# A graph layer and a 16-expert layer on one core: W centred in place of x, pads and b1 spread out, expert numbers loaded behind products

## What is computed

```python
deg = max((adj != 0).sum(-1), 1)                      # adj: 4096 x 4096, 0 or 1
xn = layernorm(x)                                     # x: 4096 x 256, over the 256, no gain or shift
x1 = x + relu((dinv * (adj + I) * dinv) @ xn @ W + xn @ W + b)   # dinv = rsqrt(deg), per row and its own degree
f = layernorm(x1)
w, idx = top_2(softmax(f @ Wr + br)); w = w / w.sum()
y = f + sum over the two chosen experts e of w_e * (gelu(f @ W1[e] + b1[e]) @ W2[e] + b2[e])
out = x1 + y
```

## Time and profile before

| | |
|---|---|
| median of 3 runs | 645.96 us |
| the profiled execution's own time | 647.67 us |
| its span, first to last instruction | 646.1 us |
| TensorE busy (products) | 585.0 us, 91% |
| VectorE busy | 456.3 us, 71% |
| ScalarE busy | 248.7 us, 38% |
| GpSimd busy | 307.2 us, 48% |
| DMA traffic | 94.60 MB, mean 146 GB/s |
| mean granted TensorE clock | 0.975 |

### The profile page before, as it was taken

The page is one execution under the profiler, slowest core; times in us unless marked ns, Lnnn a source line. Parts: engine busy times, 40 slices in busy tenths (PEclk is TensorE's granted clock), DMA queues, the critical chain, the costliest instruction groups (busy, mean ns, idle before and its releaser), DMA issues.

```text
span 646.1 us, 17010 instructions
## 1 busy us (share of the span) xinstructions
PE 585.0 (91%) x4732; PEld 459.4 (71%) x4733; DVE 456.3 (71%) x1433; ACT 248.7 (38%) x515; POOL 307.2 (48%) x348
## 2 busy tenths in 40 slices
PE   1998999999999999999717999899999999999993
PEld 1687888888888888888604666566666777777772
DVE  2664899999999999999733766667755565555662
ACT  2786343444344443444312344343332323233331
POOL 7213366666666666663320333544534443444443
PEclk9999999999999999999957999999999999999998
DMA  8916899999999999995593545666544443434320
GB/s 232 226 26 108 165 196 211 217 205 214 207 212 198 222 210 208 209 218 141 195 337 97 129 112 122 142 143 137 119 72 70 82 82 61 78 62 79 63 51 1
DMA packets 67450, 94.60 MB, mean 146 GB/s; under 512 B 9232, under 2 KB 42288, under 8 KB 66896
## 3 DMA queue, kind: packets, MB, share of 16 engines
q0 software_dynamic: 32928, 51.03, 45.6%
q1 hardware_dynamic: 32176, 40.32, 21.2%
q10 hardware_dynamic: 2304, 2.72, 1.3%
HBM read 103.71 MB, written 25.83 MB: 201 GB/s over the span
## 4 chain that ended last, share of the span: by engine, by line
PE 32%; DMA 5%; issue 5%; DVE 4%; ACT 2%; SPq 1%; POOLq 1%; DVEq 1%; POOL 0%
PE bank L584 13%; PE bank L607 11%; PE bank L592 4%; DMA out_dram<-orows,at_xg 4%; PE bank L562 2%; DVE hgs L1143 1%; ACT xseT L775 1%; PE bank L601 1%; DVE feat L1132 1%; DMA rows<-pad 1%; DMA at_xg<-rows 1%; DVE orows L1157 1%; DVE hl L1149 1%; SPq L336 0%; DVEq L1137 0%
## 5 line engine op out<-in xcount | busy, mean ns | idle before, releaser
L480 PE MATMUL bank<-wall,at_xg 128*128 128x257 f16 x1024 | 238.7, 273 | 1.9 <-DVE at_xg L842 1.6
L482 PE MATMUL bank<-wall,at_xg 128*128 128x256 f16 x1024 | 233.4, 273 | 0.0
L1322 POOL DMA_INDIRECT out_dram<-orows,at_xg x79 | 128.1, 1621 | 182.3 <-DMA out_dram<-orows,at_xg 101.2
L584 PE MATMUL bank<-wall,feat 128*128 (+1 forms) x474 | 118.0, 386 | 11.1 <-issue 8.3
L769 ACT ACTIVATE hgs<-hgs 128x512 f32<-128x512 f32 x79 | 49.8, 630 | 201.2 <-DVE hgs L1143 201.2
L1149 DVE SCALAR_TENSOR_TENSOR hl<-bank,xseT 128x512 f16<-128x512 f32 x79 | 54.6, 692 | 92.1 <-ACT xseT L775 92.1
L480 PEld LDWEIGHTS bank<-wall,at_xg 128*128 128x128 f16 x1024 | 102.9, 100 | 18.4 <-DVE at_xg L842 5.0
L1291 POOL DMA_INDIRECT rows<-feat,posi x64 | 72.7, 1136 | 85.4 <-issue 82.7
L482 PEld LDWEIGHTS bank<-wall,at_xg 128*128 128x128 f16 x1024 | 100.3, 98 | 15.3
L607 PE MATMUL bank<-wall,xseT 128*128 (+1 forms) x632 | 108.2, 273 | 0.0
L842 DVE STREAM_TRANSPOSE at_xg<-abuf 128x512 int32<-128x512 int32 x128 | 87.0, 698 | 3.9
(11 more groups left out here) (148 smaller groups left out, 768.1 us busy)
## 6 DMA issues: line engine op xcount, KB each, us to landing
abuf<-in_adj_dram POOLq DMA_DIRECT2D x128, 256.0 KB, 6.5
wst<-in_L_ffn_W_dram SPq DMA_DIRECT2D x32, 512.0 KB, 7.4
at_xg<-rows SPq DMA_DIRECT2D x79, 136.0 KB, 2.1
out_dram<-orows SPq DMA_DIRECT2D x32, 128.0 KB
abuf<-in_L_ffn_b_dram SPq DMA_DIRECT2D x4, 1024.0 KB, 9.8
wall<-in_x_dram SPq DMA_DIRECT2D x12, 256.0 KB, 13.4
rows<-pad ACTq DMA_DIRECT2D x12, 136.0 KB, 3.2
out_dram<-orows,at_xg POOLq DMA_INDIRECT x79, 3.9
```

What stands on the lines that cost most here:

```text
L480: both = [lambda: pe.matmul(ps_acc[odd][:, 0:D + 1], w, yh[:, j, 0:D + 1], start=j == 0, stop=j == T - 1), lambda: pe.matmul(ps_acc[odd][: ...
L482: lambda: pe.matmul(ps_acc[odd][:, 0:D], w, yl[:, j, :], start=False, stop=False)]
L584: mm = pe.matmul(q_h[r % 2][:, :], a, w, start=n == 0, stop=n == 3 * DC - 1)
L1322: L.indirect_dma_start(out, bass.IndirectOffsetOnAxis(ap=info[r][:, 0:1].bitcast(U32), axis=0), orow[r], None, bounds_check=N - 1, oob_is_ ...
```

## The change

First tile: x is no longer normalised before the product. TensorE makes the column means of W (`column_means`), VectorE subtracts them from W (`centre_W`), x is transposed as it arrives, and 1/sqrt of the variance multiplies y when it is copied out (`high_y`, `low_y`). Statistics run six tiles ahead (`LEAD`) in groups of 2, 3, 3 and then 4 tiles (`GROUPS`). W is the first load of SP; y has three banks in place of two; GpSimd makes the identity matrix before its first adjacency loads and issues those of tiles 1 to 3 from the first stage.

Turn: a block of pads is written early behind the start of each of the first eight experts' regions (`first_pads`), and those experts' own pads go behind their first block at the earliest (`pad_least`). GpSimd writes the pads of experts 0 to 9 and ScalarE's queue those of 10 to 15, both behind the scatters. b1 is loaded one part at a time. The last two early weight cuts are one tile earlier, the first two late weights are asked for in tile 31.

Experts: TensorE reads the number of the next block's expert after this block's first-layer products (`look_up`), except for the first block of a loop round; VectorE cuts late weights by halves, one in every block; SP asks for a block's rows before a late weight.

```diff
-PADS = ((0, 4), (4, 8), (8, 16))
+GROUPS = ((0, 2), (2, 5), (5, 8)) + tuple((n, n + 4) for n in range(8, 32, 4))
+LEAD = 6
+PADS = ((0, 10), (10, 16))
...
+    def asked_at(i):
+        return (0, 1) if isinstance(i, int) and i == T // RUN - 1 else (0, 2)
+    def cut_at(i):
+        return (1, 2) if isinstance(i, int) and i == T // RUN - 1 else (1, 3)
...
     @block.sync
+        sp.dma_start(wg_arrival, gnn_W.rearrange("(c p) n -> p c n", p=P)).then_inc(ev("w_gnn_in"), 16)
         for b in QUEUE[0]:
             load_x(sp, 0, b)
-        sp.dma_start(wg_arrival, gnn_W.rearrange("(c p) n -> p c n", p=P)).then_inc(ev("w_gnn_in"), 16)
...
-        def load_b1():
-            sp.wait_ge(ev("at_made"), T * CH)
+        def load_b1(c):
+            sp.wait_ge(ev("at_made"), (T - AB + c + 1) * CH)
...
+            if isinstance(t, int) and T - 2 <= t < T:
+                load_b1(t - T + 2)
...
+                after(sp, "pad_made", 0)
+                sp.dma_start(rows[0:U * ROOM, :].rearrange("(e r) w -> r e w", r=ROOM)[0:P, :, :],
+                             pad[:, :].unsqueeze(1).broadcast_to([P, U, RW])).then_inc(ev("first_pads"), 16)
...
+            if isinstance(t, int) and t == T - 1:
+                load_late(0)
+                load_late(1)
...
         def bstep(q, r):
-            if late(q, r) is not None and late(q, r) + 2 < 2 * (E - EARLY):
-                load_late(late(q, r) + 2)
             nxt = shift(q, r, AHEAD)
...
             if is_block(nxt, 1, 0):
                 after(sp, "table_made", 0)
                 sp.wait_ge(ev("spare_pads"), 16)
-                after_pads(sp, 2)
+                for which in range(len(PADS)):
+                    after_pads(sp, which)
             if exists(*nxt):
                 load_block(*nxt)
-        load_late(0)
-        load_late(1)
-        write_pads(sp, 0)
+            if late(q, r) is not None and r % 2 and late(q, r) + 2 < 2 * (E - EARLY):
+                load_late(late(q, r) + 2)
...
         sp.wait_ge(ev("multiplied"), T * CH)
-        after_pads(sp, 0)
         for r in range(AHEAD):
             load_block(0, r)
+        load_b1(2)
+        load_b1(3)
...
     @block.tensor
+        def column_means():
+            pe.wait_ge(ev("w_gnn_in"), 16)
+            after(pe, "one_dth", 0)
+            for c in range(DC):
+                mm = pe.matmul(ps_mean[:, 0:D], one_dth, wg_arrival[:, c, :], start=c == 0, stop=c == DC - 1)
+            mm.then_inc(ev("w_means"), 1)
         def x_T(n):
-            after(pe, "x_normed", n)
+            if n % XT == 0:
+                pe.wait_ge(x_in[n // XT], 16 * Q)
...
         def x_times_W(n):
             after(pe, "x_T_copied", n)
-            if n >= 2:
-                after(pe, "y_low", n - 2)
+            if n >= 3:
+                after(pe, "y_low", n - 3)
...
         def hidden(q, r):
-            e = expert[r] = expert_of(q, r)
-
-            pe.wait_ge(ev("w_cut"), e * 2 + 2)
+            if r == 0 and is_loop_edge(q):
+                look_up(q, r)
+            e = expert[r]
+            if isinstance(q, int) and q < LATE:
+                pe.wait_ge(ev("w_cut"), e * 2 + 2)
+            elif r == 0:
+                pe.wait_ge(ev("w_cut"), 2 * E)
...
         def expert_out(q, r):
-            e = expert[r] if r < U - 2 else expert_of(q, r)
+            e = expert[r]
...
             if exists(q, r):
                 hidden(q, r)
             if exists(*nxt):
+                if not (nxt[1] == 0 and is_loop_edge(nxt[0])):
+                    look_up(*nxt)
                 tokens_T(*nxt)
+            if r < 2 and is_loop_edge(q) and exists(*prev2):
+                look_up(*prev2)
...
     @block.scalar
         def high_y(n):
+            for g, (first, _) in enumerate(GROUPS):
+                if n == first:
+                    after(act, "rstd_made", g)
             after(act, "y_made", n)
-            act.activation(yh[:, n, 0:D], ps_Y[n % 2][:, 0:D], ACT.Copy, scale=SY).then_inc(ev("y_high"), 1)
+            act.activation(yh[:, n, 0:D], ps_Y[n % 3][:, 0:D], ACT.Identity, scale=rstd[:, n:n + 1]).then_inc(ev("y_high"), 1)
...
         act.activation(warm[:, :], mhalf[:, 0:1], ACT.Gelu).then_inc(ev("gelu_warm"), 1)
+        for odd in (0, 1):
+            act.wait_ge(listed[odd], 16 * TOPK * T // 2)
         write_pads(act, 1)
-        write_pads(act, 2)
...
-            if late(q, r) is not None:
+            if late(q, r) is not None and r % 2 == 0:
                 cut_high_late(late(q, r))
...
     @block.vector
+        def centre_W():
+            after(V, "w_means", 0)
+            for c in range(DC):
+                mm = V.tensor_tensor(wg_arrival[:, c, :], wg_arrival[:, c, :], ps_mean[:, 0:D], ALU.subtract)
+            mm.then_inc(ev("w_centred"), 1)
...
+        def cut_low_late(j, half):
+            if half == 0:
+                after(V, "w_high", 2 * EARLY + j)
+            n = DC * H // 2
...
-                cut_low_late(late(q, r))
+                cut_low_late(late(q, r), r % 2)
...
     @block.gpsimd
-            if is_(t, lambda t: t + AB - 1 < T):
+            if is_(t, lambda t: 1 <= t and t + AB - 1 < T):
                 more_adj(i, k + AB - 1, (0, 1))
...
         over_tiles(L, step)
+        write_pads(L, 0)
```

More of the change, by code:

```diff
@@ L303, in late @@
     def late(q, r):
-        return (U * q + r) // 2 if isinstance(q, int) and r % 2 and U * q + r < 4 * (E - EARLY) else None
+        return (U * q + r) // 2 if isinstance(q, int) and U * q + r < 4 * (E - EARLY) else None
     def w_dram(e, which):
@@ L327, in is_block, with is_loop_edge @@
         return isinstance(at[0], int) and at == (q, r)
+    def is_loop_edge(q):
+        return not isinstance(q, int) or q in (0, ROUNDS - 1)
     def in_table(q, r):
@@ L355, in _ @@
         for c in (2, 3):
-            for b in QUEUE[0] + QUEUE[1]:
+            for b in (0, 2, 1, 3):
                 load_x(sp, c, b)
@@ L511, in first_tile @@
                     x_T(n)
+                if n == 1:
+                    after(pe, "w_centred", 0)
                 if 0 <= n - 1 < T:
@@ L514, in first_tile @@
                 j = n - LAG
+                if j == 0:
+                    pe.wait_ge(ev("constants"), CONSTANTS)
+                    pe.matmul(ps_P[:, 0:E], ones16[:, :], firsts[:, :], start=True, stop=True)
                 if j >= 0:
@@ new lines, in centre_W, with stats_of, variance @@
+        def centre_W():
[3 more added lines that the diff above has]
+            mm.then_inc(ev("w_centred"), 1)
+        def stats_of(n):
+            if n % XT == 0:
+                V.wait_ge(x_in[n // XT], 16 * Q)
+            V.bn_stats(st6[:, n, :], xin[:, n, :]).then_inc(ev("bn"), 1)
+        def variance(g):
+            first, end = GROUPS[g]
+            cols = slice(first, end)
+            after(V, "bn", end - 1)
+            V.tensor_tensor(dif[:, cols], st6[:, cols, 1], st6[:, cols, 4], ALU.subtract).then_inc(ev("dif"), 1)
+            V.tensor_tensor(var[:, cols], st6[:, cols, 2], st6[:, cols, 5], ALU.add).then_inc(ev("var_sum"), 1)
+            after(V, "dif", g)
+            V.tensor_tensor(dif[:, cols], dif[:, cols], dif[:, cols], ALU.mult).then_inc(ev("dif2"), 1)
+            after(V, "var_sum", g)
+            V.tensor_scalar(var[:, cols], var[:, cols], 1.0 / D / SY ** 2, EPS / SY ** 2, ALU.mult, ALU.add)\
+             .then_inc(ev("var_eps"), 1)
+            after(V, "dif2", g)
+            after(V, "var_eps", g)
+            V.scalar_tensor_tensor(out=var[:, cols], in0=dif[:, cols], scalar=0.25 / SY ** 2, in1=var[:, cols],
+                                   op0=ALU.mult, op1=ALU.add).then_inc(ev("var_ready"), 1)
@@ L1158, in weigh @@
              .then_inc(ev("weighted"), 1)
-        def cut_low_late(j):
-            after(V, "w_high", 2 * EARLY + j)
-            n = DC * H
-            a, b = w_at(EARLY + j // 2, j % 2, 0), w_at(EARLY + j // 2, j % 2, 1)
-            V.scalar_tensor_tensor(out=wall[:, b:b + n], in0=wst[:, j % 2, :], scalar=SW, in1=wall[:, a:a + n],
-                                   op0=ALU.mult, op1=ALU.subtract).then_inc(ev("w_cut"), 1)
+        def cut_low_late(j, half):
+            if half == 0:
+                after(V, "w_high", 2 * EARLY + j)
+            n = DC * H // 2
+            a, b = [w_at(EARLY + j // 2, j % 2, part) + half * n for part in (0, 1)]
+            cut = V.scalar_tensor_tensor(out=wall[:, b:b + n], in0=wst[:, j % 2, half * n:(half + 1) * n], scalar=SW,
+                                         in1=wall[:, a:a + n], op0=ALU.mult, op1=ALU.subtract)
+            cut.then_inc(ev("w_cut") if half == 1 else ev("w_half"), 1)
         copy_tokens_T(0, 0)
@@ L1232, in _ @@
                    allow_small_or_imprecise_dtypes=True).then_inc(ev("constants"), 1)
-        L.memset(mhalf[:, :], -0.5).then_inc(ev("constants"), 1)
         L.memset(pad[:, :], 0.0).then_inc(ev("pad_zero"), 1)
         L.memset(feat[:, :, :, D:RW], 0.0).then_inc(ev("constants"), 1)
```

(5 more changed lines are left out.)

185 lines of the change are left out of this document (73 added, 112 removed).

## The result

The changed kernel takes 640.18 us (median of 7 runs, 638.06 to 643.06) against 646.29 beside it (7 runs): 0.9908 of the time, 95% interval 0.988 to 0.9935. It is 6.1 us faster where 18.3 were forecast, and outside the forecast range of 621 to 635. The profiled execution took 641.37, its span is 639.8 (646.1 before).

What follows compares the result with a forecast made beforehand. TensorE bound the adjacency stretch, VectorE's cycle blocks 0 to 31; time lay there and in first tile, turn and loop. 7.4 + 7.3 + 0 + 3.5 + 0.1 = 18.3 off 645.96 gave 627.7 us, range 621 to 635.

Steps and rivals of the forecast that it cites:

- Parts 1 to 5: First tile's W centring, 7.4 us, and the turn's early pads, split b1, earlier cuts and moved pads, 7.3 us.
- part 1: First tile: centring W instead of normalising x saves 7.4 us, bounds 1.9 and 9.6.
- 1.4 us of normaliser waits: First tile: TensorE's waiting for the normaliser goes, 1.4 us of the 7.4.
- The tenth tile: First tile: the tenth tile's transposes come at about 22.7, 6.0 us earlier.
- the moved cut: Turn: last early weights' cuts a step earlier take a 1.23 us cut off the last tile's path, +0.6 us.
- the slower rival: Turn to experts: GpSimd's pads take 6.0 us each and delay the first add, 667.3 us; 4%.
- chunk 0: First tile: x's first chunk taken at 9.1; rival has 11.7 and a longer low clock, 633.1 us; 8%.
- Part 7: Loop, blocks 32 to 71: expert numbers looked up behind the products save 3.5 us, bounds 0 and 5.5.
- The look-ups' 3.5: Loop: rounds of 27.65 against 28.54 us, five rounds 4.4, less 0.9 for the first round's longer branch.
- The rival that gave part 7 nothing: Loop: look-ups already run ahead of their products, so moving them gives 0, 631.2 us; 12%.
- Part 6: Blocks 0 to 31: late cuts in halves give 3.79 us a block, taken as 0, bounds -3 and +3.
- up to 1 from SP's order: Near block 17: row loads ahead of late weights in SP's order ease the stall, worth up to 1 us.

Runs made afterwards that it cites:

- e17: Kernel before with first-tile change and turn changes only; whole cuts, SP's order, look-ups and own-expert waits as before: 632.9 us.
- e7: Kernel before with only the first-tile change (W centred in place of normalising x, new order of loads, groups and lead): 642.0 us.
- e8: Kernel before with only the turn changes (early pads, b1 in pieces, moved cuts, pads on GpSimd and ScalarE): 640.1 us.
- e1: Changed kernel with each block again waiting only for its own expert's cuts, not all 32 at a round's head: 635.0 us.
- e9: Same code as e1, run again in a later submission: 637.6 us.
- e16: Same code as e1, run again as the control of the half-row adds' submission: 636.5 us.
- e18: Changed kernel as it is, run again on the chip of e17: 640.1 us.
- e4: Changed kernel with look-ups back in front of their products and each block waiting for its own expert's cuts: 635.6 us.
- e3: Changed kernel with SP's load order of before and late weights cut whole at every second block: 640.0 us.
- e2: Changed kernel with SP's order of before, a late weight's load ahead of the row load: 640.9 us.
- e13: e1's kernel with the first 16 adds adding only 64 of 128 rows, the other rows' results left out: 633.6 us.
- e14: Kernel before with the first 16 adds cut to 64 rows, the other rows' results left out: 644.6 us.
- e12: Changed kernel with late weights in steps 8 to 39, second-layer look-ups set back, loop from block 48 with the all-cuts wait: 632.9 us.

## Why the prediction was wrong, by its steps

**Parts 1 to 5: right.** 7.4 and 7.3 were forecast; block 0 starts 6.9 and 7.4 earlier with each alone, and the two together gain 14.5 of the forecast 14.7 (e17). Alone they gain only 4.7 and 6.5 in time, 11.2 in sum. The profiles have 3.3 us more than before from block 8 to 17 in e7, 0.5 in e8 and 1.5 in e17, which may be the difference, but one profile each doesn't show it. Inside part 1, 1.4 us of normaliser waits went as written: 22 tiles take 29.03 (52.31 less 23.28) against 30.45. The tenth tile came 5.4 earlier, not 6.0: the sum had no wait for VectorE's transposed adjacency rows, and TensorE stood idle 1.27 us for them at 20.44. The four products of a tile took 2.05 us at 10.20 and 1.03 from 15.96 on, so the clock rose a little before the 16.6 put for it; only these lengths tell, since the granted-clock column reads 1.00 all through the first tile in both kernels. In the turn the moved cut gave 0.4 in place of 0.6 (11.51 us from the last product to the last scatter, 11.91 before) and the way from there to block 0's rows 6.9 in place of 6.7. GpSimd's ten pads took 1.22 us each where SP's 1.24 was assumed, and were out of the way 8 us before the first add, so the slower rival is out; chunk 0 came at 8.97, so its rival too.

**Part 7: the step that failed.** The prediction counted the look-ups and overlooked that the same hunk replaces each block's wait for its own expert by one for all 32 cuts at a round's head. That it costs something could be read from the kernel before, whose last late cut ran 2.3 us past the start of block 32's first layer (465.25):

```profile
466.35 1.22 DVE L1164 SCALAR_TENSOR_TENSOR wall<-wst,wall 128x1024 f16<-128x1024 f32 x1
```

Runs e1, e9 and e16, with the old wait, gain 11.2, 9.1 and 11.4 us, where the changed kernel gains 6.1 and 7.2 (e18): about 4 us of loss in place of nothing, and the profiles have 4.0 more from block 31 to 33 (12.7 against 8.7). The look-ups' 3.5 is the second error: e4 and e1 differ by 0.6. "Behind six products of 0.22 they are covered" holds in inner steps, which fell to 3.38. But over eight even steps a round was to keep 0.55 (0.4 and 0.15), and rounds two to five kept 1.2 (28.26 less eight times 3.38), because the step with the doubled look-up is 4.09. And the base of 28.54 held the first round's extras; the four rounds after it were 28.33 before. The rival that gave part 7 nothing (631.2) was right on what the look-ups brought, but not on why: they did not stand ahead of their products, the inner steps gained and the round's head lost as much. About 4 of its remaining 9 us are the wait.

On the look-ups the trace shows 0.49 us of idle time in front of a transpose that stands behind six products, four transposes and two look-ups (518.08), and nothing that the profile shows released it, so the sequencer doesn't read far enough ahead there to hide them. The Trainium skill, Advanced Engine Details and Errata, section Sequencer Loop, lets it read on while engine instructions wait; the 0 that this rule gave for part 7 is what e4 measured, its cover isn't what the trace shows.

**Part 6: 0 was forecast, and the runs are uneven.** The pace with halves is about as forecast: e4 and e1 take 53.6 and 52.7 us from block 17 to 31, where 14 times 3.79 is 53.1; e17, with whole cuts, takes 52.4. Yet e4, parts 1 to 6, has a ratio of 0.984 (0.981 to 0.987) where e17, parts 1 to 5, has 0.977 (0.975 to 0.979): about 4 us for part 6, but on two chips, and one kernel's gain moved by up to 2.3 between chips (e1, e9, e16). Undone while part 7 stays (e3), it returned nothing. So the parts' costs don't add up, and why part 6 costs what it does is open; the share of the "up to 1 from SP's order" was tried (e2) and is nothing.

So of the 12.2 us that are missing (18.3 less 6.1), about 4 are the wait, 3.5 are the look-ups' gain that never was, and some 4 are part 6 or what it does together with the chain of adds; the last is not shown. The chain differs from one execution to the next: the two profiles of the changed kernel (first and e18) are 4.5 us apart in their spans, and 3.4 of that lies between block 8 and block 17 (39.9 against 36.5). The first two profiles, one of each kernel, could not show this.

## What to carry to other kernels

Read every wait that a hunk moves or widens as a cost of its own, and look for what its last releaser is doing at that moment in the trace of before: a wait for all of something is as late as the last one. A chain of serial DMAs half hidden under compute gives a stall whose size changes from one kernel and one execution to the next (34.5 to 42.9 us for the same nine blocks in the runs here with whole adds); compare several profiles before one stall is given a cause. And measure parts separately: here five of seven brought 14.5 us and the other two took 7 back.

## What the hardware showed that I had not expected

An indirect add of 64 rows in place of 128 shortens the chain by far less than half: the first gap of e13 is 5.69 us against 5.93 in e16, the third 4.05 against 6.13, the nine together 40.6 against 46.1, and 38.6 (e14) against 41.4 in the kernel before. The first gap was 4.7 to 4.9 us in all six profiles of kernels without part 7, and 5.45 to 6.15 in 12 of the 14 with it, though GpSimd's work is the same and in e12 no late weight was loaded then. What ties them is not found, and one profile each is little: the changed kernel itself shows 6.00 and, in e18, 4.81. After 3.7 us of idle time TensorE's granted clock was 0.50 in the window from 459 to 462, and 1.00 again from 463 to 466.
